# A constant multiplied into a free bank while TensorE waits: thirteen runs of idle-time matmuls in a perceiver layer

## The reference, cut to what matters

```python
x = x + xattn(layernorm(x), ctx, ctx)   # 16 heads of 16: q=.@Wq, k=.@Wk, v=.@Wv, softmax(q k^T) v, @ Wo
x = x + attn(layernorm(x))              # 16 heads of 64, causal, scores / 8, softmax, @ wo^T
x = x + ffn(layernorm(x))               # 256 -> 1024 -> 256, exact gelu
# in ffn: weights rounded to 8 bits per column or row, x and the hidden values to 16 bits,
# each with ONE scale: the largest magnitude over the whole tensor
```

## Time and profile before

| what | value |
|---|---|
| median of 3 runs | 707.97 us (707.05 to 709.99) |
| the profiled execution, its time | 707.11 us |
| its span, first to last instruction | 705.3 us |
| mean granted TensorE clock | 0.954 |
| busy share of the span: PE / PEld / DVE / ACT / POOL | 86% / 73% / 66% / 55% / 24% |
| cross-attention, self-attention, feed-forward | begin at 0, about 344 and about 616 us of the span |

### The profile page before, as it was taken

How to read it: one execution, slowest core, us unless ns; L and a number is a source line. 1 busy time by engine, 2 the same in 40 slices (tenths; PEclk the granted TensorE clock), 3 DMA queues, 4 the chain that set the end, 5 groups by cost and what they waited for, 6 DMA issues and landing times. The chain is left out here.

```text
span 705.3 us, 18395 instructions
## 1 busy us (share of the span) xinstructions
PE 607.5 (86%) x6678; PEld 516.0 (73%) x6678; DVE 465.1 (66%) x981; ACT 385.5 (55%) x1009; POOL 169.5 (24%) x160
## 2 busy tenths in 40 slices
PE   3389688898989898998498999999999999769697
PEld 2377577777777787876387888889897988634397
DVE  3157376767777677677569975666657474647797
ACT  3157377776768676778344142433324252347895
POOL 4341515151423233240002031212203020241000
PEclk9779899999999999999699999999999999979899
DMA  7549554656565646351030000000000000000002
GB/s 238 134 120 318 122 141 115 155 122 149 134 149 132 151 99 160 91 118 40 17 104 2 2 2 1 0 0 0 0 0 0 1 2 2 1 9 0 1 31 91
DMA packets 33865, 52.08 MB, mean 74 GB/s; under 512 B 5377, under 2 KB 13697, under 8 KB 33825
## 3 DMA queue, kind: packets, MB, share of 16 engines
q1 hardware_dynamic: 29280, 42.75, 23.8%
q10 hardware_dynamic: 4352, 8.39, 4.1%
q0 software_dynamic: 192, 0.39, 0.2%
HBM read 17.96 MB, written 2.10 MB: 28 GB/s over the span
## 5 line engine op out<-in xcount | busy, mean ns | idle before, releaser
L548 ACT ACTIVATE Pr<-pS,nmax 128x256 f32<-128x256 f32 x256 | 119.2, 476 | 61.2 <-DVE nmax L644 60.2
L644 DVE TENSOR_REDUCE nmax<-pS 128x2 f32<-128x512 f32 x128 | 87.8, 687 | 74.1 <-PE pS L405 73.3
L326 POOL TENSOR_TENSOR Qst<-Qraw,rows_of 96x1024 fp32r<-96x1024 f32 x32 | 59.9, 1891 | 93.0 <-DMA Qraw<-QSh 90.1
L415 PE MATMUL pT<-ident,Pr 128*128 128x128 f32 x512 | 77.4, 273 | 0.2 <-ACT Pr L548 0.2
L860 POOL TENSOR_TENSOR a_Pr<-a_Pr,a_rinv 128x512 f32<-128x512 f32 x32 | 32.8, 1046 | 185.8 <-DVE a_rinv L1146 185.8
L405 PE MATMUL pS<-Kst,Qst 96*128 96x256 f32 x256 | 60.1, 317 | 15.0 <-POOL Qst L326 10.3
L1026 ACT ACTIVATE a_Pr<-a_Pr 128x512 f32<-128x512 f32 x32 | 20.2, 631 | 75.9 <-DVE a_Pr L1138 75.9
L415 PEld LDWEIGHTS pT<-ident,Pr 128*128 128x128 f32 x512 | 59.6, 141 | 0.4 <-ACT Pr L548 0.4
L405 PEld LDWEIGHTS pS<-Kst,Qst 96*128 96x128 f32 x256 | 40.3, 194 | 24.9 <-issue 14.3
L555 ACT ACTIVATE PT<-pT 128x512 f32<-128x512 f32 x64 | 38.2, 598 | 28.3 <-PE pT L415 26.7
L548 ACT ACTIVATION_READ_ACCUMULATOR Pr<-pS,nmax 128x1 f32 x256 | 52.5, 205 | 0.0
(11 more groups left out here) (258 smaller groups left out, 1852.1 us busy)
## 6 DMA issues: line engine op xcount, KB each, us to landing
Kst<-KSh SPq DMA_DIRECT2D x128, 128.0 KB, 2.5
CT<-ctxT ACTq DMA_DIRECT2D x16, 512.0 KB, 4.9
Kst<-KSl SPq DMA_DIRECT2D x64, 128.0 KB, 2.5
Qraw<-QSh SPq DMA_DIRECT2D x60, 64.0 KB, 2.0
X<-x SPq DMA_DIRECT2D x4, 512.0 KB, 8.7
out<-X SPq DMA_DIRECT2D x8, 256.0 KB, 2.1
Qraw<-QSl SPq DMA_DIRECT2D x30, 64.0 KB, 2.0
raw<-awq SPq DMA_DIRECT2D x1, 1024.0 KB, 6.7
```

The lines of the kernel that those rows point to most:

```text
L326: last = pool.tensor_tensor(Qst[r][:, :, :, :, h2, :].rearrange("p j g a q -> p (j g a) q"), Qraw[:, :, r].rearrange("p j g a q -> p j (g ...
L415: last = pe.transpose(pT[s % 2][:, t, k, :], Pr[s % 2][:, t, P * k:P * k + P], ident[:, :])
L548: act.activation(Pr[c % 2][:, t, :], pS[c % 2][:, t, :], ACT.Exp, bias=nmax[c % 2][:, t:t + 1], accum_out=rsum[par][:, c // 4, 2 * (c % 4) ...
L644: dve.tensor_reduce(nmax[s % 2][:, :], pS[s % 2][:, :, :], AX.X, ALU.max, negate=True).then_inc(maxed, 1)
```

## The change

A helper `keep_busy(pe, n, bank, identb, causal)` issues n matmuls of 128x512 in bf16, identity times mask, into a bank that nobody reads before it is overwritten. It waits for nothing and signals nothing. It is called at thirteen places in TensorE's order, 138 matmuls in all: 22 ahead of the first product, 32 ahead of the first scores, 5, 3 and 5 in the end of the cross-attention, 18 and 8 in the beginning of the self-attention, and 8, 3, 6, 6, 7 and 15 in the feed-forward. No other engine's program changes.

```diff
+def keep_busy(pe, n, bank, identb, causal):
+    for _ in range(n):
+        pe.matmul(bank, identb[:, :], causal[:, :, :], start=True, stop=True, skip_group_check=True)
...
+            def spare(n):
+                keep_busy(pe, n, pO[:, :, :, :, :].rearrange("p g b a q -> p (g b a q)"), identb, causal)
+
             pe.wait_ge(consts, CONSTS)
+            spare(22)
             for r, (kind, ahead, part) in enumerate(AHEAD):
                 if kind != "X":
                     pe.wait_ge(w_lo, W_ORDER.index("QKV".index(kind)) + 1)
                 if r == 6:
+                    spare(32)
                     score(0, 0)
                     score(0, 1)
                 project(r, r, kind, part, ahead, 3)
...
             weigh(QUADS - 1, 14, True)
+            keep_busy(pe, 5, pJ[0][:, :], identb, causal)
             turn_o(PAIRS - 1)
+            keep_busy(pe, 3, pJ[0][:, :], identb, causal)
             turn_back(PAIRS - 1)
+            keep_busy(pe, 5, pJ[0][:, :], identb, causal)
             project_out(PAIRS - 1)
...
+            keep_busy(pe, 18, pO[0][:, :, :].rearrange("p j n -> p (j n)"), identb, causal)
             for k, (kind, part) in enumerate(AHEAD):
+                if k == 2:
+                    keep_busy(pe, 8, pO[0][:, :, :].rearrange("p j n -> p (j n)"), identb, causal)
...
                 last.then_inc(w_turned, 1)
+                keep_busy(pe, 8 if k == 0 else 3, bank[0][:, :], identb, causal)
                 pe.wait_ge(w_copied, k + 1)
...
             spread_max(0)
+            keep_busy(pe, 6, bank[0][:, :], identb, causal)
...
             turn(0)
+            keep_busy(pe, 6, bank[0][:, :], identb, causal)
...
             steps(pe, hidden)
+            keep_busy(pe, 7, bank[HB][:, :], identb, causal)
             spread_max(1)
+            keep_busy(pe, 15, bank[HB][:, :], identb, causal)
```

More of the change, by code:

```diff
@@ L90, in build @@
         self_attention(nc, X, ident, identb, causal, half, raw, raw_in, ffn, w_inT, w_out)
-        feed_forward(nc, X, ident, identb, half, ffn, b_in, b_out, out)
+        feed_forward(nc, X, ident, identb, causal, half, ffn, b_in, b_out, out)
 class Ffn:
@@ L1268, in _, with feed_forward @@
             steps(dve, body)
-def feed_forward(nc, X, ident, identb, half, ffn, b_in, b_out, out):
+def feed_forward(nc, X, ident, identb, causal, half, ffn, b_in, b_out, out):
     G = 512
```

## The result

| | before | changed |
|---|---|---|
| median of 20 runs each, us | 709.08 | 704.0 |
| their spread, us | 706.3 to 711.7 | 700.8 to 707.9 |
| ratio, with its 95% interval | | 0.993 (0.9916 to 0.9945) |
| span of the profiled execution, us | 705.3 | 703.5 |
| mean granted clock of TensorE in it | 0.954 | 0.981 |

The changed kernel is 5.0 us faster (4 to 6). I had summed 5.25, and 702.3 us for the median; it is 704.0. Of the 1.7 us between them 1.1 come from the starting point: the kernel before has a median of 709.08 over 20 runs, and I had worked from 707.97 over 3. A second set of runs, later and beside the kernel before, gave 0.9939 (0.992 to 0.9958). The total agrees; the parts agree less well.

What follows compares the result with a forecast made beforehand. TensorE was taken to work at half clock behind waits that the change cannot shorten. Gains of 0.6 + 0 + 2.0 + 2.4 + 0.25 = 5.25 us gave 701.9 or 702.7, stated as 702.3 us, range 699.2 to 706.0.

Steps and rivals of the forecast that it cites:

- The price of a constant: Everywhere: one 128x512 bf16 constant takes 0.216 us at full clock and 0.44 at half clock.
- The 22, 0.6 us: Ahead of the first product: faster first K lets ScalarE's second copy start sooner, gaining 0.6 us (bounds 0 and 0.65).
- only the second copy, at 16.96, waits for TensorE: First K: ScalarE's first copy waits on GpSimdE, its second on TensorE and could start at 16.31, 0.65 us sooner.
- on which the first scores hang in the end: Start: the first scores depend on the first K's 12 DMAs, so an earlier K, 0.6 us, brings them sooner.
- The 32, nothing: Ahead of the first scores: clock falls again in the 3.3 us idle behind them, gain 0 (other end 2.7 us).
- rival A: Start of cross-attention: clock also holds until the second pair's K, 2.7 us more gain, 699.6 us; chance 0.16.
- The border, 2.0: Last cross-attention tile and self-attention start: faster output, Q and K products gain 2.0 us (ends 0 and 2.2).
- The feed-forward, 2.4: Feed-forward's turn and first hidden products run at full clock, gaining 2.4 us (ends 0 and 2.9).
- its end, 0.25: Around the second maximum: VectorE paces the end, so faster w_out products gain only 0.25 us (ends 0 and 2.0).
- The sixes (1.3 each) under waits of 1.4: Feed-forward: each run of six constants takes 1.3 us and fits inside a wait of 1.4 us.
- C: Everywhere: constants do not lift the clock and are slow themselves, about 19 us lost, 726 us; chance 0.09.
- B: Self-attention start, feed-forward and head: engines behind TensorE take gain back, leaving 2.5 us, 705 us; chance 0.25.

Runs made afterwards that it cites:

- Border only: Kernel before plus only the 5, 3, 5, 18 and 8 constants where cross-attention meets self-attention; ratio 0.996 to the kernel before.
- without the 22: Changed kernel minus its first 22 constants, ahead of the first K; 705.05 us, ratio 0.9948 to the kernel before.
- feed-forward only: Kernel before plus only the 8, 3, 6, 6, 7 and 15 constants of the feed-forward; ratio 0.9949 to the kernel before.
- more in the cross-attention: Changed kernel with 11 constants added ahead of the first transposes, 6 ahead of Q, 44 for the 32, 6 after the first scores; 701.27 us, ratio 0.9907.
- head only: Kernel before plus only the 22 constants ahead of the first K and 32 ahead of the first scores; 710.19 us, ratio 1.0011.
- more in the feed-forward: Changed kernel with 11 and 5 constants in place of the 8 and 3 at the feed-forward's start; 702.28 us, ratio 0.9921.
- the 88: Changed kernel with its first 22 constants of 512 columns replaced by 88 of 128 columns; 704.61 us, ratio 0.994.
- everything together: Changed kernel with 88 short constants for the 22, more in the cross-attention (51 for the 32), and 11 and 5 in the feed-forward; 701.22 us, ratio 0.9896.
- the next wait as well: The kernel of everything together plus 24 constants ahead of the fourth pair's K in the loop's first round; 700.71 us, ratio 0.99.

## Why the prediction came out right, and where it did not

**The price of a constant** (0.216 and about 0.44): right. 15 take 3.41 us and 22 take 6.41, the first of them at half clock.

**The 22, 0.6 us:** wrong. In the changed kernel's profile ScalarE's second copy of K does come sooner, from ScalarE's timeline,

```profile
15.72 1.08 ACT L550 ACTIVATE KSh<-pJ 128x512 fp32r<-128x512 f32 x2 [4.20 <-POOL rows_of L348]
```

two copies in a row instead of one at 15.71 and one at 16.96, and SyncE begins to lay K out at 17.75, 0.64 sooner than 18.39. Two steps failed. The first is "only the second copy, at 16.96, waits for TensorE": it does so in some executions only. Border only and without the 22 have no constants ahead of K, and yet ScalarE's two copies stand in a row,

```profile
15.34 1.19 ACT L548 ACTIVATE KSh<-pJ 128x512 fp32r<-128x512 f32 x2 [4.13 <-POOL rows_of L348]
```

(border only), and SyncE begins 2.02 and 2.03 us after the first copy, as in all nine with constants. Only before (2.68) and feed-forward only (2.63) have the wait. In border only TensorE's products reach the faster pace at 14.8 us, before at 16.5; without the 22, GpSimdE released ScalarE only at 16.06. The second is "on which the first scores hang in the end": they do, but through SyncE's queue, which in the changed kernel carries

```profile
25.66 0.56 SPq L263 DMA_DIRECT2D Qraw<-QSh  x1
26.27 1.67 SPq L263 DMA_DIRECT2D Qraw<-QSl  x1
```

one DMA of 1.67 in place of 0.60. From the start of K's layout to GpSimdE's masked Q it takes 32.09 - 17.75 = 14.34 us; before it took 31.65 - 18.39 = 13.26. The 0.64 gained is more than eaten, and the first scores start at 35.97. A K that is done sooner also leaves TensorE idle sooner: the clock fell at about 17.6 us and not at 20.0, and VectorE began Q's low part at 22.88, not 22.27. But that is not on the path: it was done at 23.57, and SyncE takes up Q's DMAs only at 25.66, right behind those of K. With it done at 22.15, in the kernel with more in the cross-attention, the masked Q comes no sooner.

**The 32, nothing:** right in the total, for the reason given. The clock fell at 38.0, behind 2.96 us without work, a few scores and 1.61 more, as it did behind 3.64 in the row I leaned on the earlier trace rows. Quite nothing it is not: from K's first product to the next scores it takes 4.31 us in the changed kernel and 5.25 before, since the clock rises again sooner. With the same 32 other profiles have 4.2 to 5.25, and head only shows that no gain arrives that can be told. What I did not see is that this was a matter of number: more of them, with a start that ends early enough, hold it, and that is rival A.

**The border, 2.0:** 2.5 in the profiles, 2.8 +- 1.6 by the runs, somewhat over my upper end of 2.2. Sixteen Q and K products at 0.12 do what was said, 1.6. That the 18 end late and VectorE's weight split hides it is right too, with 0.8 late and not 0.4. What I sized too small is the last tile of the cross-attention, 0.4: its rows are ready 9.79 - 8.88 = 0.9 us sooner.

**The feed-forward, 2.4, and its end, 0.25:** F fell by 88.69 - 85.8 = 2.9 us where the clock held (2.65 predicted), by 1.2 in the first profile, where it did not. Here the Trainium skill (TensorE: Matmul & The Clock Gate, Part 4: PE-mode transpose) has the full clock not engage for transposes. The eight of the turn take 1.09 us behind six fast constants (more in the feed-forward) and 1.99 in the earlier trace rows: transposes behind other work run at the full clock, and there the measurement decides against the page. Whether transposes alone would raise a fallen clock no run here shows. I had not priced that the six could be slow themselves. "The sixes (1.3 each) under waits of 1.4" assumes a clock that is still full when they begin, and in front of them stand ScalarE's copies, which a late load of b_in can push back, and two short waits for the maximum. So in the changed kernel's first profile one of my signs did not come: the first hidden product starts 11.35 us behind the first transposes, before 10.65, and 9.71 in the second profile.

**The end stage's pace:** right. The gain of the 7 and 15 is small, the 15 fast (3.41) and the w_out products behind fast, while VectorE goes on to set the end; I did not separate their part by an experiment of its own, but the profiles do: from the first w_out product to the first finished tile added it is 9.15 to 9.28 us in the three without these constants and 8.95 in the ten with them, 0.2 to 0.3 for the 0.25 I took.

**The rivals.** C (the constants do not lift the clock) is refuted by the 6.41 us of the 22. B (the engines behind TensorE take the gain back) does not hold at the border or in the feed-forward, where the lengths shrank in full; in the head nothing of a gain arrives, and for the second quad it is open. So the 5.25 was right in total with one term, 0.6, gone and the others 0.5 and, with the clock held, 0.25 larger: that these cancel is luck.

**The signs.** One that I had named for being wrong came true: the first scores start later than 35.5. It was badly chosen, for they did so in the kernel before as well (35.54). The first Q product at 351.80 also misses "by 350.4", because the cross-attention of that execution was longer. The clock of 1.00 from slice 19 on, the 0.12, and the second copy right behind the first at about 16.3 came; of the two slow stretches of the feed-forward, only the second was at 1.00 throughout.

On the size of such gains, the Trainium skill (TensorE: Matmul & The Clock Gate, What's actually happening) puts the cost of the warm-up below 1% of a typical kernel's span. The best version here gained 1.04% (0.8 to 1.3), 7.4 us; the page's figure and the measurement can't be told apart. But the page speaks of the ramp from a cold start, and this gain came from waits all along the kernel, not from the first products: the 22 ahead of them earned nothing that can be told. So the 7.1 us that I derived from it were no bound on what can be won here.

## What to carry to other kernels

Take the slices of the granted clock, then the waits in front of each slow stretch: only where the work behind a wait is itself on the path does a run of constants pay. Size it by the wait at full clock. What is too long costs nearly one for one as soon as no other engine's work covers it, and if the clock has already fallen when the run begins, it lasts twice as long. A run that is too short leaves a gap in which the clock can fall again, and then it only moves the slow stretch. So look in the changed profile whether the clock is still full at the end of the gap, not only whether the constants ran. Then follow the gained time through the next queue, for another engine's layout DMAs may keep it.

## What the hardware showed that I had not expected

A DMA issue on SyncE's queue now and then takes about 1 us longer than its like (0.45 to 1.45), and in each profile where I looked at such an issue there was one packet of the instruction queue, 0.02 MB, within a microsecond or so of it: before at 63 us, changed kernel at 26 and 90, more in the cross-attention at 23, the 88 at 21. Two rows of SyncE's queue, of the kernel before and of the one with more in the cross-attention:

```profile
63.24 2.21 SPq L257 DMA_DIRECT2D Qraw<-QSh  x2
```

```profile
23.54 2.39 SPq L292 DMA_DIRECT2D Kst<-KSh  x2
```

Pairs of this kind otherwise take 1.25. And the packet's line in the changed kernel's view of the DMA queues, for 26 to 27 us (packets, MB, their time as a share of 16 engines' stretch):

```profile
q8 instruction: 1, 0.02, 7.5%
```

The path from K's layout to the masked Q takes 13.2 to 13.5 us in the six kernels without a packet between 17 and 30 us (before, border only, feed-forward only, without the 22, everything together, and the next wait as well) and 13.9 to 14.4 in the seven with one. In each of the seven exactly one issue or pair of SyncE's is long at that packet, by 0.45 us where the path takes 13.93, and by 0.8 to 1.15 where it takes 14.1 to 14.4. Only TensorE's program differs between these kernels, and the packet of 42 or 43 us in the three without the head's constants stands at 39 with the 32 alone, at 21 to 26 in the seven, and at 14, with a next one at 37 or 38, in the two with the most. So it is probably TensorE's program text. So adding instructions, even ones that do nothing and lie in a wait, moves these fetches into or out of a queue that is on the path. That the one causes the other is inferred from the coincidence in thirteen profiles; I made no experiment that moves the packet and nothing else.
